# Preparing the expert factors of a layer every third slot instead of every second

## The reference

```python
h = _L0_tok_ref(x, ...)                       # tanh layers and a strided convolution: 375 rows
h = h + _L0_attn_ref(_layernorm(h), ...)      # retention with rotary positions
h = h + _L0_ffn_ref(_layernorm(h), ...)       # product keys, below, and causal attention over 8 heads
h = h + _L1_attn_ref(_layernorm(h), ...)      # one gradient step of a small network, then its output
h = h + _L1_ffn_ref(_layernorm(h), ...)       # 8 experts, the best one taken

# in _L0_ffn_ref, per head (8) and row (375):
sim = jnp.einsum('pbnhd,pkhd->pbnhk', q, pk_keys)      # two lists of 64 scores
scores, idx = jax.lax.top_k(sim, 16)
... final_scores, pk_idx = jax.lax.top_k(score, 16)    # the best 16 of the sums
k = jnp.einsum('bnhk,bnhkd->bnhd', kv_scores, keys_table[ind])      # 16 of 4096 rows
v = jnp.einsum('bnhk,bnhkd->bnhd', kv_scores, values_table[ind])
```

## Time and profile before

| | us |
|---|---|
| median of 3 runs | 6543.29 (6541.79 to 6549.09) |
| the profiled execution, its own time | 6530.81 |
| span of the profile | 6529.0 |
| busy: PE, ACT, POOL, DVE | 5693.9 (87%), 4642.1 (71%), 4415.3 (68%), 4115.3 (63%) |
| mean granted clock of TensorE, share of full speed | 0.964 |

### The profile page before, as it was taken

One profiled execution on the slowest core, in us unless ns is written; L12 is line 12 of the kernel. 1 busy time (PEld: TensorE's weight loads), 2 busy tenths in 40 slices (PEclk: granted clock), 3 DMA queues, 4 the chain that ended last, 5 costly groups with the idle time before them and its releaser, 6 DMA issues.

```text
span 6529.0 us, 79900 instructions
## 1 busy us (share of the span) xinstructions
PE 5693.9 (87%) x24704; PEld 3145.4 (48%) x24704; DVE 4115.3 (63%) x13330; ACT 4642.1 (71%) x10889; POOL 4415.3 (68%) x4108
## 2 busy tenths in 40 slices
PE   2699898988989898988989888898989889899977
PEld 1345454544545454454545445454544545454533
DVE  7665757747585774758567474857647485762157
ACT  1577777767777776777777777777777777777833
POOL 0486867859586785968678585867768596777700
PEclk9999999999999999999999999999999999999978
DMA  1111111111111111111111111111111111111100
GB/s 35 39 55 41 49 47 44 52 36 55 39 52 45 43 55 36 52 42 49 45 46 51 39 52 38 50 47 47 51 36 52 38 55 42 46 50 46 47 21 15
DMA packets 93462, 290.43 MB, mean 44 GB/s; under 512 B 17879, under 2 KB 26546, under 8 KB 92780
## 3 DMA queue, kind: packets, MB, share of 16 engines
q1 hardware_dynamic: 92748, 285.25, 13.4%
q10 hardware_dynamic: 288, 0.07, 0.0%
HBM read 280.68 MB, written 4.61 MB: 44 GB/s over the span
## 4 chain that ended last, share of the span: by engine, by line
PE 60%; POOL 16%; ACT 15%; DVE 6%; issue 2%; DMA 0%; SPq 0%; DVEq 0%; ACTq 0%
PE accu L520 27%; POOL dense_w L449 16%; PE dense L528 9%; PE dense L506 7%; ACT dense L910 4%; ACT dense_w L904 3%; PE sims L641 2%; PE work L647 2%; PE work L568 1%; PE work L685 1%; PE dense L494 1%; PE work L634 1%; PE work L621 1%; PE dense L816 1%; ACT prob_odd L978 1%
## 5 line engine op out<-in xcount | busy, mean ns | idle before, releaser
L449 POOL TENSOR_TENSOR dense_w<-dense_w,store 128x375 f32<-128x375 f32 x4096 | 4412.9, 1098 | 1786.2 <-ACT dense_w L904 1746.1
L520 PE MATMUL accu<-dense_w,store 128*128 128x375 f32 x8192 | 3369.9, 494 | 227.9 <-POOL dense_w L449 162.2
L910 ACT ACTIVATE dense<-dense 128x375 f32<-128x375 f32 x4096 | 1917.5, 468 | 909.7 <-PE dense L528 682.0
L904 ACT ACTIVATE dense_w<-dense 128x375 f32<-128x375 f32 x4096 | 1965.1, 480 | 217.9 <-PE dense L506 216.2
L520 PEld LDWEIGHTS accu<-dense_w,store 128*128 128x128 f32 x8192 | 1449.1, 196 | 568.1 <-issue 203.0
L528 PE MATMUL dense<-store,hot 128*128 128x375 bf16 x4096 | 1347.6, 330 | 254.9 <-ACT dense_w L904 253.3
L506 PE MATMUL dense<-store,spread 96*128 96x375 bf16 x4096 | 1355.7, 331 | 13.9 <-ACT dense L910 11.2
L528 PEld LDWEIGHTS dense<-store,hot 128*128 128x128 bf16 x4096 | 397.8, 97 | 1129.8 <-ACT dense_w L904 710.6
L506 PEld LDWEIGHTS dense<-store,spread 96*128 96x128 bf16 x4096 | 403.9, 99 | 806.8 <-ACT dense L910 533.7
L1294 DVE TENSOR_TENSOR picks<-codes,keys 125x4096 uint16<-125x4096 uint16 x192 | 501.0, 2610 | 7.4 <-ACTq L897 1.9
L1302 DVE TENSOR_REDUCE store<-picks 125x256 bf16<-125x2048 uint16 x192 | 438.9, 2286 | 6.6
(11 more groups left out here) (256 smaller groups left out, 6047.6 us busy)
## 6 DMA issues: line engine op xcount, KB each, us to landing
store<-in SPq DMA_DIRECT2D x513, 512.0 KB, 3.3
x_in<-in SPq DMA_DIRECT2D x16, 187.5 KB, 2.4
store<-in SPq DMA_DIRECT2D x1, 2048.0 KB, 8.9
queries_kept<-n3T SPq DMA_DIRECT2D x16, 93.8 KB, 3.4
h_saved<-h SPq DMA_DIRECT2D x16, 93.8 KB
store<-queries_kept SPq DMA_DIRECT2D x16, 93.8 KB, 2.4
store<-h_saved SPq DMA_DIRECT2D x16, 93.8 KB
out<-store SPq DMA_DIRECT2D x16, 93.8 KB
```

Of the source, the lines that this page charges most:

```text
L449: nc.gpsimd.tensor_tensor(dense_w[:, i % RING, :], dense_w[:, i % RING, :], first_of[:, i // CHUNKS, :], ALU.mult).then_inc(s["weighed"], 1)
L520: last = mm(accu[:, 0, 0:S], table[:, n % PIECE_RING, i % PIECE, :], dense_w[:, i % RING, :], start=(c == 0), stop=(c == CHUNKS - 1))
L904: fn(dense_w[:, i % RING, :], dense[:, ORDER.step[i] % BANKS, 0:S], ACT.Relu, scale=-1.0).then_inc(s["taken"], 1)
L910: fn(here, here, ACT.Relu, scale=FAR).then_inc(s["past"], 1)
```

## The change

A constant is changed. After head 1's factors (slots 0, 2, 4, 6 before; 0, 3, 6, 9 after), the 24 later ones are turned in slots 30, 32, ... 76 before and in slots 30, 33, ... 99 after.

```diff
 SPREAD_LAG, SUM_LAG, RING = 2, 6, 6
 SLOTS = STEPS + SUM_LAG
 FACTORS = 4
-PREPARED_EVERY, LATER_FROM = 2, 30
+PREPARED_EVERY, LATER_FROM = 3, 30
```

## The result

The changed kernel took 6593.22 us (median of 20 executions, 6547.72 to 6639.40) against 6541.69 us (20, 6533.19 to 6549.20) for the kernel before in the same rounds: a ratio of 1.0062, 95% interval 1.0046 to 1.0078. It is slower by about 0.6%, 40 us. (The two medians lie 51.5 us apart, a quotient of 1.0079; the executions of the changed kernel fall into groups, and the quotient of the two means is 1.0061.) The forecast was 6523 us, faster, with a range of 6480 to 6585 us; both missed.

The account below looks back on a forecast made before the run. Tight slots (PE waiting for ACT's take, then ACT for PE), DVE's chain and POOL slowed by DVE were taken as bounds. 1.33 - 0.5 + 1.0 - 3.2 = -1.4 us per image, x 14 = -20: 6543 to 6523 us (6480 to 6585).

Parts of the forecast that it names:

- The pace of the slots: Each factor makes two slots tight at 1.28 us; a loose slot takes 0.95 us, so a bf16 factor costs 0.66 us.
- the sum of tight slots: Over 24 factors both versions pay the same 17.9 us per image; only the place where it is paid changes.
- the 5.3 of the seven factors: Slots 77 to 98: seven factors with two f32 surcharges make them 5.3 us longer, less 0.5 hidden under POOL.
- the factors under POOL: Slots 87 to 99: five factors stand where POOL runs without pause; 0 to 3.3 us hidden, 0.5 taken.
- PE's wait for line 1400: End of the gradient: shorter slots 62 to 68 only make PE wait longer for DVE, about 1.3 us.
- the saving of slots 30 to 76: Eight of 24 factors leave these slots: 5.96 us less per image, of which 1.33 us are not had.
- DVE's wait for the last factor: Before the first ranks_of: DVE waits about 10 us per image, falls 4.7 us behind the slots, costed at nothing directly.
- the carry of POOL's backlog: After slot 99: three later ranks_of come 4.7 us later, backlog moves into PE's pauses; gain 0 to 3.9 us, 3.2 taken.
- the lost pause: The first ranks_of leaves the pause of soften and starts behind slot 99; 0 to 2.27 us lost, 1.0 taken.
- The rival's 6593 us: Rival: one more drop of TensorE's granted clock in slots 77 to 99, 5 us an image, 6593 us; chance 0.06.
- The uncovered case: Rival: factors come uncovered and no backlog is carried; 2.8 us per image slower, 6582 us; chance 0.22.
- the saving of slots 62 to 68: Gradient slots before line 1400 get 1.33 us shorter, lost in PE's wait for DVE; bounds 0 and 2.0 us.

Follow-up runs that it names:

- `wait_later`: The changed kernel with DVE's wait for factors_out moved behind the first ranks_of; 6496.49 us against 6530.75, ratio 0.9948 to the kernel before.
- The wait alone: The kernel before with factors_out raised by ACT in slot 99, the factors staying in slots 30 to 76; 6556.39 us against 6530.75, ratio 1.0039.
- `soften_later`: The changed kernel with ACT's soften of the first tile behind slot 99 instead of slot 97; 6539.80 us against 6530.75, ratio 1.0012.
- `more_fill`: The changed kernel with two slots more in the gradient stretch ending at PE's wait for line 1400; 6549.16 us against 6536.90, ratio 1.0020.
- both moves: The changed kernel with DVE's wait behind the first ranks_of and the nine-slot gradient fill; 6489.74 us against 6536.90, ratio 0.9926.
- `head1_only`: The kernel before with only head 1's factors moved to slots 0, 3, 6, 9; 6518.68 us against 6536.90, ratio 0.9974.

## Why the prediction was wrong

**Right.** The pace of the slots: two tight and one loose, 1.28, 1.28 and 0.95 us; the sum of tight slots is the same. Slots 77 to 98 cost 5.5 us, the 5.3 of the seven factors; the factors under POOL hid nothing of the half microsecond I gave them. PE's wait for line 1400 grew, by 41 us over the run with the weight loads counted; in the image shown PE itself waits 1.35 us, as the 1.33 said. At full clock the saving of slots 30 to 76 is 3.9 us in place of 4.6: 2.1 of the 5.96 us are not had, the upper bound that the prediction gave, and not the 1.33 it took. DVE's wait for the last factor was forecast at 10 us an image and is 11.4. Its first `ranks_of` falls behind the slots as forecast: it starts 3.88 us before slot 98's `past` in the kernel before and 0.61 us behind it in the changed one, 4.5 us where 4.7 was forecast:

```profile
3387.16 2.56 DVE L1294 TENSOR_TENSOR picks<-codes,keys 125x4096 uint16<-125x4096 uint16 x1 [11.37 <-ACTq L897]
```

**Wrong: the carry of POOL's backlog.** The prediction said of DVE's wait "I cost the wait at nothing directly", since every instruction that waits for DVE had slack, and then that POOL's backlog, coming later, would be "carried into later pauses of PE", a gain of 3.2 us less 1.0. The slack was there: line 1343 still waits 532.0 us in all. The gain of 3.2 us was not. With slot 99's own 0.66 taken off, slots 98 to 190 got 1.7 us longer in the image shown (2.4 at full clock) where I had 2.2 us shorter, and `wait_later` shows that the delay of DVE costs 3.4 us of an image in that stretch. The wait alone, put into the kernel before, costs 0.39%; the wait shortened in the changed kernel turns 1.0062 into 0.9948. This step alone is worth about 4 us an image or 55 us, more than the whole distance of 29 us between forecast (6523) and the profiled execution's 6552.

The error in the reasoning was to count PE's pauses (1.08, 1.40 and 1.40 us) as free time of POOL. POOL was working in them already: between slots 98 and 190 of the kernel before it idles 2.5 us in four gaps, none above 0.73. A backlog that comes later finds less than 3.2 us to be worked off in. Cut at the pauses, the image shown has slots 98 to 133 1.4 us longer than before (0.66 is the factor of slot 99, and 1.0 had been put down for the lost pause), slots 133 to 160 0.9 us shorter, and slots 160 to 190 1.8 us longer. Only the middle one shows anything like a carry, and the next one takes about twice as much back.

What the profiles show besides is that the passes of `ranks_of` stood well where they were: the first began in the pause of `soften`, in which PE stands anyway and POOL had a backlog to work off. Behind slot 99 it falls on slots that PE could use, and POOL idles 3.37 us in that pause. Against `wait_later`, where the first pass is back in its place, the changed kernel loses 2.2 us in slots 98 to 133 (44.4 and 42.2) and 1.2 us in slots 133 to 190 (70.7 and 69.5). So about two thirds of the loss lie beside the first tile's passes and one third beside the second tile's. That the lost pause itself, and not the delay of the other three sets, makes most of the first part is argued; `soften_later`, which gives that pause back, recovers part of the loss, but no run separates the two.

**The clock.** The rival's 6593 us is the measured median almost to the microsecond, by luck: the drop of the clock that it put in slots 77 to 99 did not come. The windows of the changed kernel by stage (slots 77 to 98 and 98 to 190; length, busy times of PE, PEld, DVE, ACT and POOL with counts, granted clock, DMA share, GB/s):

```profile
3356.50:3386.50 30.00, 25.93 (x117) 12.57 (x114) 19.01 (x104) 24.68 (x54) 20.95 (x21) 1.00 0.16 54
3386.50:3501.60 115.10, 97.31 (x385) 51.00 (x386) 101.35 (x246) 83.43 (x194) 111.84 (x93) 0.99 0.16 55
```

Slots 77 to 98, now mostly tight, show 1.00 (that is 2.4 GHz), in this image and in the other 13. The rule that the prediction weighed (the Trainium skill, TensorE: Matmul & The Clock Gate, section "A second HAM failure mode: psum-queue depth-cycling") would have it swing there; this image does not show it.

The same window of the kernel before, slots 98 to 190, and that of `wait_later` behind it:

```profile
3382.10:3494.80 112.70, 100.51 (x381) 52.82 (x382) 93.73 (x245) 82.72 (x193) 109.59 (x94) 0.94 0.17 56
```

```profile
3361.80:3473.40 111.60, 98.11 (x385) 51.84 (x386) 91.37 (x243) 83.15 (x194) 106.70 (x93) 0.97 0.17 56
```

The changed kernel's clock is the higher one there, 0.99 against 0.94, its PE is busy 3.2 us less, and the stretch still takes 2.3 us longer: PE idles, and the clock is not the cause. POOL is busy 2.3 us longer on one multiplication less, and 5.1 us longer than in `wait_later` on the same number. DVE's 7.6 us more are in part the first set of passes, which stood ahead of slot 98 before.

The clock does decide which group an execution falls into, and these lie 40 us apart; the median landed in the middle one. The prediction's own sign of being wrong, a granted clock that differs from 0.964 by over 0.01, came true in the profiled execution (0.977) and not in those near the median (0.966). At that clock, near the one of the kernel before, the changed kernel takes 6593 to 6605 us, some 50 us more.

**The uncovered case**, 6582 us at 0.22, had the mechanism nearest to what happened. Its three conditions held: the saving of slots 62 to 68 was lost in DVE's wait, the first `ranks_of` lost its pause, and nothing net was carried, where the prediction had set the border at "the carry is below about 1.8 us". That its 6582 us equal 6541.69 x 1.0062 is in part luck: it puts down 2.8 us an image, and the loss at an equal clock is about 4.6.

## What to carry to other kernels

A wait with slack behind it is not free if the work it moves slows another engine: ask what runs beside the delayed work now, and what ran beside it before. When a resource is released later (here a buffer by its last reader), look for the part of the waiting work that doesn't need it and move the wait behind that part; here this turned a loss of 0.6% into a gain of 0.5%. And compare profiles stage by stage at fixed points of the program: the totals hid a stage that gained 6 us and two that lost 8. Read the granted clock of each stretch with its length: here it made the gain look 2.4 us larger than it is (6.3 and 3.9), and the growth of a wait for POOL 5 us larger (6.4 and 1.4).

## What the runs showed that I had not expected

- The same program's executions can differ by 90 us (6547.72 to 6639.40) with the granted clock between 0.977 and 0.957, while kernels that differ from it in a fill, a wait or the places of the last factors kept within 5 to 17 us (over 5 to 11 executions each): 6540.37 to 6557.07 for `more_fill`, 6484.99 to 6495.93 for both moves. Why is open.
- A stage of the attention at full clock takes the same time to 0.2 us in three kernels, and costs up to 5 us more in images where the clock falls in it. A difference of 0.2% can so come from where the clock falls alone: `head1_only` won 0.26%, and at full clock none of its stages is shorter than before by more than 0.2 us.
- POOL's multiplication takes 0.84 us at best, 0.98 at the median and up to 3.09 beside DVE's passes. Not every pass does it. In the kernel before, a multiplication that starts while line 1294 runs takes 2.9 us at the median, and one that starts within line 1299 takes 1.95 us; both lines read two operands. Nine in ten of these end 0.71 to 0.84 us after DVE's instruction does, as if they only began then. Beside line 1302, a reduction with one operand and 2.3 us long, they take 0.85 us. DVE waits too: line 1294 takes 2.28 us when POOL is idle at its start and 2.75 at the median when a multiplication is running.
- POOL's total hardly moves with the place of these passes (4412.9 and 4428.5 us), the program's time does.
